# Four chained transformer layers on one core: another order and another way of loading in the two wide cross attentions

## The chip, the cores and the metric

The kernel runs on one core of one Trainium2 chip. The metric is the device time of one execution in microseconds (us), the median of several runs. A core has five engines that each work through their own list of instructions in order and wait for one another by semaphores: TensorE (PE; its weight loads are listed apart as PEld), VectorE (DVE), ScalarE (ACT), GpSimd (POOL) and SyncE (SP), which here only issues DMAs.

## The reference

Two sequences x of 1024 tokens by 256 features go through four layers; each layer has a self attention, a cross attention to 77 context tokens of 192 features, and an MLP. Layers 0 and 1 have 16 heads of 16 features ("narrow"), layers 2 and 3 have 16 heads of 64 ("wide"). In layer 2 a rope turns queries and keys. The part in which the change lies is the wide cross attention:

```python
def _attn(xq, ctx, wq, wkv, wo, bo):       # layer 2; layer 3 is the same without _rope
    q = _heads(xq @ wq)                    # 16 heads x 1024 x 64
    k, v = jnp.split(ctx @ wkv, 2, axis=-1)
    k = _heads(k); v = _heads(v)           # 16 heads x 77 x 64
    q = _rope(q, sq, cq)
    k = _rope(k, sk, ck)
    sim = jnp.einsum('bhnd,bhmd->bhnm', q, k) * DH ** (-0.5)
    a = jax.nn.softmax(sim, axis=-1)
    o = jnp.einsum('bhnm,bhmd->bhnd', a, v)
    return o.transpose(0, 2, 1, 3).reshape(xq.shape[0], xq.shape[1], MID) @ wo + bo
```

All is float32; products are made of split operands (a high and a low part, stacked along the contraction).

## The kernel before

The whole program is one launch. A planner, not the text of the program, sets the order. Every stage (one self attention, cross attention, key and value preparation "kv", or MLP of a layer) calls `plan.put(at, end, steps)`, where `at` is a time in the stage's own units; all steps of a stage are sorted by it, and then each engine's program is written by going through the one list and doing, for each step, what that engine has in it. So every engine works in the order of the list, and a step that waits holds up whatever stands behind it on that engine. Results of TensorE lie in PSUM banks, which are taken in turn from a small ring and given back by the engine that reads them.

**A unit of a wide cross attention.** `core64_steps` (its first loop) writes the steps of 32 units n. One unit is two heads times 512 queries:

- `cs` n, 0 and n, 1: scores of one head each, eight matmuls (L939, 128x256, the two heads of a pair). VectorE takes the maximum (L1716), ScalarE four exponentials of 128x77 with their sums (L1402).
- `cnorm` n: VectorE's reciprocal of the sums (L1725) and GpSimd's multiplication of all the unit's weights by it (L1939, 128x616).
- `cturn` n: TensorE transposes them (L1043, eight), ScalarE copies them out of PSUM (L1410, 77x1024).
- `cav` n: weights times values (L1055); `fin` n: ScalarE copies the output (L1391, 128x512).
- `proj` n: output projection (L1161, eight matmuls for a unit); VectorE adds it to x (L1769).

Before, their places relative to n are -1, -0.6, -0.3, 0.15, 0.65, 0.66 and 1.35.

**Queries.** Beside the units, `nat64` makes the queries of a group g of four heads, in two halves of 12 matmuls (L939, 128x512). There are eight groups; two of them are made ahead of the units, six among them, one for each four units (at 4g - 6.7 to 4g - 5.3). In layer 3 ScalarE copies such a block out of PSUM (L1335, high part) and VectorE forms its low part (L1631). In layer 2 it is turned by the rope first: ScalarE copies (L1347), VectorE multiplies by the cosine (L1644), GpSimd by the sine (L1926) and adds and subtracts the halves (L1932, L1933), ScalarE writes the high part (L1353) and VectorE the low one (L1651). `qstack` then moves the parts by DMAs of SyncE (L2102) into the stacks QS, of which there are three. `w_load` (L2002) brings a group's weights to a staging buffer and `w_split` (L1572, L1576 on VectorE) splits them.

**Keys and values.** The kv stage of layer 2 runs beside the MLP of layer 1, that of layer 3 beside the MLP of layer 2. It puts keys to DRAM as KXD (`kv_keep`, L2125, 616-byte rows) and values as VD (L2131). At the start of the cross attention `kv_stack` (L2136, L2143, L2147) loads from there the two key stacks KXA and KXB_, in which one key's parts are repeated on other partitions, and the values. In KXB_ a head uses half of the partitions and the other half has to be zero; VectorE clears it in `begin64` (L1595, L1596) after clearing parts of the query stacks (L1588, L1592) and the tail of the key tiles (L1594), and SyncE waits for that before L2143. TensorE waits for all key pieces (`kx_in`) before the first scores.

**Rope table.** `rope_load` (L2016) loads the table in layer 2 twice, once for the self attention and once for the cross attention into its own tile `S.CS`.

The lines that do the loading, before:

```python
for blk, s in enumerate((0, 1, 0, 1)):
    e.dma_start(f(S.KXA[32 * blk:32 * blk + 32, :, 0:NW]), KXD[s].rearrange("(h r) n -> r h n", r=32)
                ).then_inc(*kx_in.inc(S.i, 16))
w.wait_ge(zeroed, (S.i, "k"))
```

The norm of the following MLP (`norm_steps`, L1320, L1549, L960 and others) stands among the last units of each sequence.

## Time and profile before

| | |
|---|---|
| median of 3 runs | 4787.32 us (4774.97 to 4794.02) |
| profiled execution, its own time | 4777.17 us |
| its span in the profile | 4775.4 us |
| mean granted TensorE clock | 0.936 |
| busy: PE, DVE, ACT, POOL | 4153.2, 3084.2, 2077.1, 1344.1 us (87, 65, 43, 28%) |
| cross attention of layer 2 | about 2824 to 3207 us of the span |
| cross attention of layer 3 | about 4287 to 4620 us |

The profile is of one execution; times in it are microseconds from the span's start. In the rows below, a row of the timeline gives start, duration, engine, line, operation, what is written and read with its shape, how many instructions were put together (x8), and in brackets how long the engine was idle before and which instruction of which engine ended that. PEclk is the clock that TensorE was granted, as a share of the full 2.4 GHz; its lower level is 1.2 GHz. A wait is put down to the last releaser.

### The profile page before, as it was taken

What the parts mean: (1) busy time and instruction counts of PE and PEld (TensorE: products, weight loads), DVE (VectorE), ACT (ScalarE), POOL (GpSimd) and SP (SyncE); (2) the same over time, 40 slices, a digit from 0 to 9 for tenths busy, and PEclk for the clock granted to TensorE, in tenths of its full rate; (3) what the DMA queues carried; (4) which work ended last, traced back from release to release, by engine and by line L of the source; (5) the groups of instructions that cost most, each with busy time, mean ns of one, the idle gap of its engine ahead of it and who ended that gap; (6) DMA issues with size and microseconds to landing.
All of it is one profiled execution on the core that took longest, in us unless ns stands there. A gap on an engine that the chain in (4) does not pass through costs nothing. (4 is left out here: it accounts for less than half of the span.)

```text
span 4775.4 us, 56539 instructions
## 1 busy us (share of the span) xinstructions
PE 4153.2 (87%) x20828; PEld 2555.2 (54%) x20828; DVE 3084.2 (65%) x4628; ACT 2077.1 (43%) x3756; POOL 1344.1 (28%) x664
## 2 busy tenths in 40 slices
PE   6899989799998888888989877779799999987879
PEld 4343356634335665554555435658555555545668
DVE  4888856688885655666666754335577777773345
ACT  2555644255564433333333434544244344434541
POOL 1000001100001024555555543321243444441120
PEclk9999989899998989999999988889899999998989
DMA  4223231212323122221222224321322232226420
GB/s 120 31 52 47 42 56 34 49 28 48 45 42 61 33 60 66 56 58 40 62 62 58 59 67 92 86 64 32 81 70 67 59 69 62 57 42 135 91 60 18
DMA packets 155299, 282.01 MB, mean 59 GB/s; under 512 B 36186, under 2 KB 68244, under 8 KB 153872
## 3 DMA queue, kind: packets, MB, share of 16 engines
q1 hardware_dynamic: 155024, 278.40, 27.8%
q8 instruction: 166, 2.72, 0.2%
q14 instruction: 109, 0.89, 0.1%
HBM read 101.01 MB, written 25.23 MB: 26 GB/s over the span
## 5 line engine op out<-in xcount | busy, mean ns | idle before, releaser
L939 PE MATMUL PS<-t 128*128 128x512 f32 (+4 forms) x7896 | 2015.5, 387 | 232.0 <-ACT t L1381 99.3
L939 PEld LDWEIGHTS PS<-t 128*128 128x128 f32 (+2 forms) x7896 | 1264.1, 188 | 792.5 <-issue 256.2
L1381 ACT ACTIVATE t<-PS 128x512 f32<-128x512 f32 (+2 forms) x1600 | 1164.5, 750 | 1083.3 <-PE PS L939 1076.9
L1659 DVE TENSOR_REDUCE t<-PS 128x1 fp32r<-128x1024 f32 x512 | 621.8, 1220 | 304.1 <-PE PS L1011 298.1
L1119 PE MATMUL PS<-t 128*32 128x512 f32 (+2 forms) x4352 | 813.0, 613 | 0.2
L1663 DVE TENSOR_REDUCE t<-PS 128x1 f32<-128x512 f32 x1024 | 649.1, 682 | 76.1 <-PE PS L1015 74.7
L1952 POOL TENSOR_TENSOR t<-t 128x1024 f32<-128x1024 f32 x256 | 621.1, 2426 | 144.7 <-ACT t L1381 119.7
L1015 PE MATMUL PS<-t 96*128 96x512 bf16 x1024 | 375.0, 396 | 37.4 <-DMA t<-scr_n 13.5
L1011 PE MATMUL PS<-t 128*128 128x512 f32 x1024 | 339.4, 415 | 59.3 <-DMA t<-t 40.6
L1948 POOL TENSOR_TENSOR t<-t 128x1024 f32<-128x1024 f32 x64 | 155.5, 2430 | 743.4 <-PE PS L1129 462.7
L1890 POOL TENSOR_TENSOR t<-t 128x2048 f32<-128x2048 f32 x24 | 109.4, 4559 | 893.2 <-DMA t<-in_rows 560.4
L1119 PEld LDWEIGHTS PS<-t 128*32 128x32 f32 (+2 forms) x4352 | 171.2, 122 | 329.9 <-issue 325.6
L1161 PE MATMUL PS<-t 128*128 128x256 f32 x1024 | 282.4, 425 | 27.7 <-ACT t L1402 11.6
L1015 PEld LDWEIGHTS PS<-t 96*128 96x128 bf16 x1024 | 97.2, 97 | 374.7 <-DVE t L1663 155.9
L1769 DVE TENSOR_TENSOR t<-PS,t 128x1024 f32<-128x1024 f32 x128 | 156.4, 1222 | 211.1 <-PE PS L1161 211.1
L1011 PEld LDWEIGHTS PS<-t 128*128 128x128 f32 x1024 | 197.1, 197 | 125.4 <-DVE t L1659 31.7
L1161 PEld LDWEIGHTS PS<-t 128*128 128x128 f32 x1024 | 214.9, 216 | 70.2 <-issue 20.4
L1402 ACT ACTIVATE t<-PS,t 128x77 f32<-128x77 f32 x512 | 159.3, 324 | 182.2 <-DVE t L1716 182.2
L1748 DVE RECIPROCAL PS<-PS 128x256 f32<-128x256 f32 x128 | 224.7, 1755 | 12.5 <-PE PS L1129 12.5
L1249 PE MATMUL PS<-t 128*128 128x256 f32 x1536 | 217.1, 293 | 13.3 <-DVE t L1864 4.6
L1249 PEld LDWEIGHTS PS<-t 128*128 128x128 f32 x1536 | 205.9, 198 | 25.8 <-issue 10.1
L1939 POOL TENSOR_TENSOR t<-t 128x616 f32<-128x616 f32 x64 | 78.2, 1222 | 447.0 <-DVE t L1725 447.0
(135 smaller groups left out, 3982.0 us busy)
## 6 DMA issues: line engine op xcount, KB each, us to landing
t<-t SPq DMA_DIRECT2D x512, 128.0 KB, 3.6
t<-t SPq DMA_DIRECT2D x256, 256.0 KB, 3.9
t<-scr_n SPq DMA_DIRECT2D x288, 128.0 KB, 6.2
scr_n<-t SPq DMA_DIRECT2D x72, 256.0 KB, 2.2
t<-t SPq DMA_DIRECT2D x256, 64.0 KB, 2.0
t<-in_L_Wg SPq DMA_DIRECT2D x16, 768.0 KB, 4.6
t<-in_L_W SPq DMA_DIRECT2D x36, 256.0 KB, 3.2
t<-in_L_Wo SPq DMA_DIRECT2D x64, 128.0 KB, 2.6
```

The source lines that it names most:

```text
L939: ins = e.matmul(out, l, r, start=i == 0, stop=i == len(terms) - 1, tile_position=tp)
L1011: ins = e.matmul(o[:, 512 * h:512 * h + 512], u.smq[j][qt], u.smk[j][h], start=True, stop=True)
L1015: e.matmul(o, u.smq[j][qt], u.smk[j][half], start=True, stop=True).then_inc(*bank_full[k].inc(nth))
L1119: ins = e.matmul(banks[S.ot][wd * j:wd * j + wd, :], u.v[j][kt], P[0:S.pr, j, :], start=kt == 0, stop=kt == S.nkt - 1, tile_position=(0, w ...
L1161: ins = e.matmul(o[:, 256 * q:256 * q + 256], S.OR[n % 2][:, 128 * q:128 * q + 128], u.wo[:, :], start=True, stop=True)
L1249: ins = e.matmul(banks[4 + q][:, 0:D], l, r, start=m == 0 and t == 0, stop=m == 7 and t == 2)
L1381: e.activation(dst, src, ACT.Exp, scale=S.L.scale).then_inc(*expd.inc((S.i, i)))
L1402: ins = e.activation(S.PQ[n % 3][:, j, t, :], o[:, 256 * t + CT * b:256 * t + CT * b + CT], ACT.Exp, bias=S.NM[n % 3][:, at], accum_out=S. ...
L1659: e.tensor_reduce(S.MT[m % 2][:, qt, j:j + 1], o, AX.X, ALU.max, negate=True).then_inc(*bank_free[k].nth(nth))
L1663: e.tensor_reduce(S.NMX[:, 4 * j + qt, half:half + 1], o, AX.X, ALU.max).then_inc(*bank_free[k].nth(nth))
L1748: e.reciprocal(o[:, hs], o[:, hs]).then_inc(*recip_made.inc((S.i, n, h)))
L1952: e.tensor_tensor(S.AP_[:, :, :], S.AP_[:, :, :], P[1][:, :, :], ALU.add).then_inc(*pool_summed.inc((S.i, n, kt)))
```

## The change

Four things change.

1. The places of a unit's steps in both wide cross attentions become -1.25, -0.85, -0.45, 0, 0.5, 0.51 and 0.9.
2. In layer 2 the cross attention uses the rope table tile of the self attention, which is now laid out so that the tile survives; it is loaded once, and that load waits for the new signal `kx_stacked`. Tiles of the cross attentions move in SBUF for it.
3. The key stacks are put together in DRAM: a new step `kv_restack` at 14.2 of the kv stage copies KXD to KXAD and KXBD (eight DMAs from DRAM to DRAM, and in layer 2 two more that write zeros into KXBD from a small tile; layer 3 uses the same zeros). `begin64` no longer clears KXB_.
4. `kv_stack` is four steps, for heads 0 to 4, 5 to 8, 9 to 12 and 13 to 15, at -19.5, -8.9, 1 and 4. Each loads a slice of the two stacks from DRAM (all 128 partitions in one DMA); the first and the last also load the values of one sequence. `kx_in` is four signals and `vx_in` two, so that a unit waits for its own piece.

```diff
+    KXAD, KXBD = dram("scr_ka", (128, 16, 2 * CT)), dram("scr_kc", (128, 16, 2 * CT))
...
+            if L.rope:
+                C.CS, C.roped = first.CS, first.i
...
-            for at, step in ((-1, ("cs", S, u.n, 0)), (-0.6, ("cs", S, u.n, 1)), (-0.3, ("cnorm", S, u.n)),
-                             (0.15, ("cturn", S, u.n)), (0.65, ("cav", S, u.n)), (0.66, ("fin", S, u.n)),
-                             (1.35, ("proj", S, u.n, 0))):
+            for at, step in ((-1.25, ("cs", S, u.n, 0)), (-0.85, ("cs", S, u.n, 1)), (-0.45, ("cnorm", S, u.n)),
+                             (0, ("cturn", S, u.n)), (0.5, ("cav", S, u.n)), (0.51, ("fin", S, u.n)),
+                             (0.9, ("proj", S, u.n, 0))):
...
+        plan.put(14.2, 0, [("kv_restack", K)])
...
-                    if L.rope:
-                        plan.put(-19.8, 0, [("rope_load", S)])
-                    plan.put(-19.5, 0, [("kv_stack", S.kv)])
+                    for i, at in enumerate((-19.5, -8.9, 1, 4)):
+                        plan.put(at, 0, [("kv_stack", S.kv, i)])
...
-                kv_ready(w, S)
+                kv_ready(w, S, u.pi % 8 // 2)
...
-                w.wait_ge(vx_in, S.kv.i)
+                w.wait_ge(vx_in[u.part.b], S.kv.i)
...
                     for k in K.keys:
-                        e.memset(f(k[:, 16 * NW:16 * NW + 102]), 0.0)
-                    e.memset(f(K.KXB_[0:64, 1::2, :]), 0.0)
-                    e.memset(f(K.KXB_[64:128, 0::2, :]), 0.0).then_inc(*zeroed.inc((K.i, "k")))
+                        ins = e.memset(f(k[:, 16 * NW:16 * NW + 102]), 0.0)
+                    ins.then_inc(*zeroed.inc((K.i, "k")))
...
             elif what == "kv64_stats":
                 S, = a
+                e.memset(S.Z[:, :], 0.0).then_inc(*k_zero.inc(S.i))
...
             elif what == "rope_load":
                 S, = a
-                if not S.cross:
-                    K = kvs[S.L.i]
-                    w.wait_ge(kx_kept, K.i)
-                    for v in vx_kept:
-                        w.wait_ge(v, (K.i, 1))
+                K = kvs[S.L.i]
+                w.wait_ge(kx_stacked, K.i)
+                for v in vx_kept:
+                    w.wait_ge(v, (K.i, 1))
...
-            elif what == "kv_stack" and a[0].L.style == 64:
+            elif what == "kv_restack":
                 S, = a
+                if S.L.i == 2:
+                    w.wait_ge(k_zero, S.i)
+                    z = S.Z[:, :].rearrange("p (o n) -> p o n", o=1).broadcast_to([64, 8, 2 * CT])
+                    for odd in range(2):
+                        e.dma_start(KXBD[64 * odd:64 * odd + 64, 1 - odd::2, :], z).then_inc(*kx_stacked.inc(S.i, 16))
                 w.wait_ge(kx_kept, S.i)
                 for blk, s in enumerate((0, 1, 0, 1)):
-                    e.dma_start(f(S.KXA[32 * blk:32 * blk + 32, :, 0:NW]), KXD[s].rearrange("(h r) n -> r h n", r=32)
-                                ).then_inc(*kx_in.inc(S.i, 16))
-                w.wait_ge(zeroed, (S.i, "k"))
+                    e.dma_start(KXAD[32 * blk:32 * blk + 32, :, :], KXD[s].rearrange("(h r) n -> r h n", r=32)
+                                ).then_inc(*kx_stacked.inc(S.i, 16))
                 for blk, s in enumerate((2, 3)):
                     for odd in range(2):
                         src = KXD[s].rearrange("(h two r) n -> two r h n", two=2, r=32)[odd]
                         at = 32 * blk + 64 * odd
-                        e.dma_start(f(S.KXB_[at:at + 32, odd::2, :]), src).then_inc(*kx_in.inc(S.i, 16))
-                for i in range(2):
-                    w.wait_ge(vx_kept[i], (S.i, 1))
-                for b in range(NB):
-                    e.dma_start(S.VXS[b][:, :], VD[b]).then_inc(*vx_in.inc(S.i, 16))
+                        e.dma_start(KXBD[at:at + 32, odd::2, :], src).then_inc(*kx_stacked.inc(S.i, 16))
+            elif what == "kv_stack" and a[0].L.style == 64:
+                S, i = a
+                w.wait_ge(kx_stacked, S.i)
+                hs = slice((0, 5, 9, 13)[i], (5, 9, 13, 16)[i])
+                for K, D_ in ((S.KXA, KXAD), (S.KXB_, KXBD)):
+                    e.dma_start(f(K[:, hs, :]), D_[:, hs, :]).then_inc(*kx_in[i].inc(S.i, 16))
+                if i % 3 == 0:
+                    b = i // 3
+                    for j in range(2):
+                        w.wait_ge(vx_kept[j], (S.i, 1))
+                    e.dma_start(S.VXS[b][:, :], VD[b]).then_inc(*vx_in[b].inc(S.i, 16))
```

Lines after the change are 8 to 9 higher than before from L939 on (L1043 is L1052, L1161 is L1170, L1402 is L1411).

TensorE in layer 2, around the first query block of a group, from the transposes of one unit to those of the next. L1043 are the transposes, L939 with 128x256 scores, L939 with 128x512 the query block, L1055 the values, L1161 the projection. Before:

```order
L1043 MATMUL PS<-t 77x128 x8
L939 MATMUL PS<-t 128x512 x12
L1161 MATMUL PS<-t 128x256 x4
L939 MATMUL PS<-t 128x256 x8
L1055 MATMUL PS<-t 64x512 x2
L939 MATMUL PS<-t 128x256 x8
L939 MATMUL PS<-t 128x512 x12
L1043 MATMUL PS<-t 77x128 x8
```

After:

```order
L1052 MATMUL PS<-t 77x128 x8
L948 MATMUL PS<-t 128x256 x8
L948 MATMUL PS<-t 128x512 x12
L1064 MATMUL PS<-t 64x512 x2
L948 MATMUL PS<-t 128x256 x8
L1170 MATMUL PS<-t 128x256 x4
L1052 MATMUL PS<-t 77x128 x8
L948 MATMUL PS<-t 128x512 x12
```

The second scores now stand ahead of the first query block, the projection behind the next scores, and the second block behind the next transposes.

ScalarE in layer 2, at the two query blocks of the last group. L1347 is the copy of a query block, L1353 its high part after GpSimd's work, L1402 the exponentials of a head, L1410 the copy of the transposes, L1391 the copy of a unit's output. Before:

```order
L1410 ACTIVATE t<-PS 77x1024
L1347 ACTIVATE t<-PS 128x2x512
L1402 ACTIVATE t<-PS,t 128x77 x4
L1353 ACTIVATE t<-t 128x2x512
L1391 ACTIVATE t<-PS 128x512
L1402 ACTIVATE t<-PS,t 128x77 x4
L1347 ACTIVATE t<-PS 128x2x512
L1410 ACTIVATE t<-PS 77x1024
L1353 ACTIVATE t<-t 128x2x512
L1402 ACTIVATE t<-PS,t 128x77 x4
L1391 ACTIVATE t<-PS 128x512
```

After:

```order
L1419 ACTIVATE t<-PS 77x1024
L1411 ACTIVATE t<-PS,t 128x77 x4
L1356 ACTIVATE t<-PS 128x2x512
L1400 ACTIVATE t<-PS 128x512
L1362 ACTIVATE t<-t 128x2x512
L1411 ACTIVATE t<-PS,t 128x77 x4
L1419 ACTIVATE t<-PS 77x1024
L1356 ACTIVATE t<-PS 128x2x512
L1411 ACTIVATE t<-PS,t 128x77 x4
L1362 ACTIVATE t<-t 128x2x512
L1400 ACTIVATE t<-PS 128x512
```

The exponentials of the second head stand ahead of the first block's copy now, and the output copy of a unit stands behind the second block's high part.

SyncE at the start of layer 3's cross attention. scr_k, scr_ka and scr_kc are the keys in DRAM, scr_v the values, in_L_Wo the projection's weights, in_L_caWq those of the queries. Before:

```order
L2136 DMA t<-scr_k 32x16x154 x4
L2143 DMA t<-scr_k 32x8x154 x4
L2147 DMA t<-scr_v 77x1024 x2
L2063 DMA t<-in_L_Wo 128x256 x2
L2002 DMA t<-in_L_caWq 128x512
```

After:

```order
L2161 DMA t<-scr_ka 128x770
L2161 DMA t<-scr_kc 128x770
L2166 DMA t<-scr_v 77x1024
L2071 DMA t<-in_L_Wo 128x256 x2
L2011 DMA t<-in_L_caWq 128x512
```

Three DMAs take the place of ten ahead of the projection's weights; the rest is loaded later.

## Rows read from the trace of the kernel before

**Rows 1.** Windows, TensorE: stretch, PE busy (instructions), PEclk, DMA share, GB/s

```profile
2880.00:3200.00 320.00, 253.58 (x1273) 0.88 0.34 76
4330.00:4600.00 270.00, 227.47 (x1224) 0.92 0.41 89
```

**Rows 2.** Waits, TensorE in layer 2 (2800 to 3220): total, times, longest

```profile
PE PS L1043 <- POOL t L1939: 54.4, 23, 8.4
PE PS L1161 <- ACT t L1402: 11.6, 6, 1.9
```

**Rows 3.** Waits of TensorE in layer 3 (4240 to 4640)

```profile
PE PS L1043 <- POOL t L1939: 41.2, 24, 3.4
```

**Rows 4.** Timeline of TensorE, one unit of layer 3

```profile
4431.81 1.10 PE L1043 MATMUL PS<-t 128*77 128x128 f32 x8 [1.48 <-POOL t L1939]
4432.75 1.89 PE L1161 MATMUL PS<-t 128*128 128x256 f32 x8
4434.29 1.33 PE L939 MATMUL PS<-t 128*128 128x256 f32 x8
4435.55 1.08 PE L1055 MATMUL PS<-t 77*64 77x512 f32 x4
4436.56 1.24 PE L939 MATMUL PS<-t 128*128 128x256 f32 x8
4439.30 1.10 PE L1043 MATMUL PS<-t 128*77 128x128 f32 x8 [1.50 <-POOL t L1939]
```

**Rows 5.** Timeline of VectorE, ScalarE and GpSimd ahead of the transposes at 4431.81

```profile
4428.34 0.47 DVE L1716 TENSOR_REDUCE t<-PS 128x4 f32<-128x308 f32 x1
4428.84 0.33 ACT L1402 ACTIVATE t<-PS,t 128x77 f32<-128x77 f32 x1 [2.31 <-DVE t L1716]
...
4430.06 0.61 ACT L1391 ACTIVATE t<-PS 128x512 f32<-128x512 f32 x1
4430.26 0.20 DVE L1725 RECIPROCAL t<-t 128x8 f32<-128x8 f32 x1 [1.46 <-issue]
...
4430.54 1.21 POOL L1939 TENSOR_TENSOR t<-t 128x616 f32<-128x616 f32 x1 [6.70 <-DVE t L1725]
```

**Rows 6.** Timeline of ScalarE and GpSimd, first query block of a group in layer 2

```profile
3024.12 1.02 ACT L1347 ACTIVATE t<-PS 128x1024 f32<-128x1024 f32 x1 [1.81 <-PE PS L939]
...
3025.22 2.37 POOL L1926 TENSOR_TENSOR t<-t 128x1024 f32<-128x1024 f32 x1 [5.13 <-ACT t L1347]
...
3030.22 1.22 POOL L1939 TENSOR_TENSOR t<-t 128x616 f32<-128x616 f32 x1
```

**Rows 7.** Timeline of TensorE in the same group of layer 2, its waits

```profile
3034.52 3.27 PE L1161 MATMUL PS<-t 128*128 128x256 f32 x8 [1.93 <-ACT t L1402]
...
3044.33 1.14 PE L1043 MATMUL PS<-t 128*77 128x128 f32 x8 [3.07 <-POOL t L1939]
...
3053.50 1.10 PE L1043 MATMUL PS<-t 128*77 128x128 f32 x8 [1.53 <-POOL t L1939]
```

**Rows 8.** Timeline of SyncE and TensorE, start of layer 3's cross attention

```profile
4296.80 1.78 SPq L2143 DMA_DIRECT2D t<-scr_k  x4
...
4300.34 0.42 SPq L2002 DMA_DIRECT2D t<-in_L_caWq  x1
...
4309.26 10.30 PE L939 MATMUL PS<-t 128*128 128x512 f32 x40 [14.60 <-DVE t L1572]
```

**Rows 9.** Timeline of GpSimd and VectorE, start of layer 2's cross attention

```profile
2830.82 2.34 POOL L1926 TENSOR_TENSOR t<-t 128x1024 f32<-128x1024 f32 x1 [22.08 <-DMA t<-in_rope]
...
2833.49 1.23 DVE L1644 TENSOR_TENSOR t<-PS,t 128x1024 f32<-128x1024 f32 x1
```

**Rows 10.** Timeline of SyncE and VectorE beside the MLP of layer 1

```profile
1669.28 3.40 SPq L2125 DMA_DIRECT2D scr_k<-t  x4
...
1691.44 0.36 SPq L2016 DMA_DIRECT2D t<-in_rope  x1
...
1725.23 1.28 DVE L1644 TENSOR_TENSOR t<-PS,t 128x512 f32<-128x512 f32 x2
```

More of the change, by code:

```diff
@@ L261, in _build @@
     kx_kept = signal("kx_kept")
-    kx_in = signal("kx_in")
-    vx_in = signal("vx_in")
+    kx_stacked = signal("kx_stacked")
+    k_zero = signal("k_zero")
+    kx_in = [signal(f"kx_in{i}") for i in range(4)]
+    vx_in = [signal(f"vx_in{i}") for i in range(2)]
     vx_kept = [signal(f"vx_kept{i}") for i in range(2)]
@@ L344, in attention_tiles @@
                 S.P = [sbt(c, [128, S.nh, 512]) for _ in range(S.npb)]
+            if L.style == 64 and cross:
+                S.nnq, S.nqs, S.qw = 2, 3, N
+                S.NQ = [sbt(c, [128, 4, N], F32R) for _ in range(S.nnq)]
             S.OR = [sbt(c, [128, 512]) for _ in range(2)]
+            if L.rope and cross:
+                sbt(c, [128, 196])
+                sbt(c, [128, 2, N])
             S.R = [sbt(c, [128, 4, S.nh]) for _ in range(2)]
@@ L373, in attention_tiles @@
             if cross:
-                S.nnq, S.nqs, S.qw = 2, 3, N
-                S.NQ = [sbt(c, [128, 4, N], F32R) for _ in range(S.nnq)]
                 S.QS = [sbt(c, [128, 2, 2, S.qw], F32R) for _ in range(S.nqs)]
-                if L.rope:
-                    S.CS = sbt(c, [128, 2, N])
             elif not L.rope:
@@ L409, in kv_tiles @@
                 S.CS = sbt(c, [128, 2, 2 * CT])
+                S.Z = sbt(c, [64, 2 * CT])
                 S.T4 = [sbt(c, [128, 2 * CT]) for _ in range(4)]
@@ L467, in wide_layer @@
             attention_tiles(first, c)
+            first.roped = first.i
         with ExitStack() as c:
@@ L725, in _build @@
                     for at, step in ((7.9, "kv_load"), (9.1, "kv16"), (9.15, "kv_keep"), (9.9, "kv_stack")):
-                        plan.put(at, 0, [(step, K)])
+                        plan.put(at, 0, [(step, K) + ((0,) if step == "kv_stack" else ())])
                     if not L.i:
@@ L744, in _build @@
                 if S.cross:
-                    if L.rope:
-                        plan.put(-19.8, 0, [("rope_load", S)])
-                    plan.put(-19.5, 0, [("kv_stack", S.kv)])
+                    for i, at in enumerate((-19.5, -8.9, 1, 4)):
+                        plan.put(at, 0, [("kv_stack", S.kv, i)])
                 if S.cross:
@@ L919, in m_chunk, with kv_ready @@
         return stage, hi[:, at[0], at[1]], lo[:, at[0], at[1]], at
-    def kv_ready(w, S):
-        w.wait_ge(kx_in, S.kv.i)
+    def kv_ready(w, S, i):
+        w.wait_ge(kx_in[i], S.kv.i)
         w.wait_ge(zeroed, (S.kv.i, "k"))
@@ L1020, in tensor_program @@
                     w.wait_ge(s, key)
-                kv_ready(w, S)
+                kv_ready(w, S, 0)
                 o, k, nth = take(w, ring, ("max", S.i, m, j, q0))
@@ L1635, in vector_program @@
                 i = rope_order(S).index((S, g, qk, half))
-                w.wait_ge(rope_in, S.i)
+                w.wait_ge(rope_in, S.roped)
                 w.wait_ge(rope_copied, (S.i, i))
@@ L2166, in sync_program @@
             elif what == "kv_stack":
-                S, = a
+                S, _ = a
                 w.wait_ge(kx_kept, S.i)
```

5 lines of the change are left out of this document (2 added, 3 removed).

## The prediction

> **What bounds the kernel now.** I read the windows first: in the two wide cross attentions (layer 2, 2880 to 3200 us, and layer 3, 4330 to 4600) TensorE is busy 253.6 of 320 us and 227.5 of 270, at a mean granted clock of 0.88 and 0.92 [rows 1]. Then the waits: TensorE waits for GpSimd's L1939 before the transposes of L1043 for 54.4 us in layer 2 and 41.2 in layer 3, and in layer 2 for ScalarE's exponentials before the projection for 11.6 [rows 2, 3]. The timeline shows one unit n of layer 3: transposes of n, projection of n-1, second scores of n+1, values of n, first scores of n+2, then an idle 1.50 [rows 4]. The starts are 0.94, 1.54, 1.26, 1.01 and 1.24 apart, so a unit is 5.99 of work in a period of 7.49. The idle time is a latency: behind the second scores come max 0.5, four exponentials 1.4, reciprocal 0.3 and L1939 1.27, by the starts in [rows 5], against only values and first scores (2.25) on TensorE. So these stages are bound by TensorE plus this chain; the narrow layers, self attentions and MLPs aren't touched, except that a DRAM restack is put beside two MLPs.
>
> **The change, part by part.**
>
> *Longer lead.* In the new order the projection also lies between second scores and their transposes: values 1.01, first scores 1.24, projection 1.54 = 3.8 on TensorE against a chain of 3.3 to 3.5: the wait of a plain unit goes. What is late next: the projection of n needs L1391's copy of its output, which stands on ScalarE behind the exponentials of n+1. Max 0.5, exponentials 1.3, copy 0.6 [rows 5] end 2.4 after the second scores; TensorE gets there after 2.25. New wait 0.15 to 0.2 per plain unit.
>
> Layer 3: the units of a group (two blocks of 12 query matmuls each) need one more: VectorE does L1631 behind ScalarE's copy of the same 1024 elements (1.2 us like L1644 in rows 9, and 1.0 like L1347 in rows 6) before the max of the second scores, so exponentials end 3.9 after them and the copy 4.5 where TensorE is there after 2.25 plus the time before; followed, 1.25 per group. Six groups x 1.25 = 7.5, 24 plain units x 0.17 = 4; removed 41.2 [rows 3], but 3.4 of it belong to the start below, so the steady part is -37.8 + 11.5 = -26.3. For the layer norm that runs beside the last units I take -3.4, an estimate: its chain has less waiting between units to be spread over; bounds 0 and -7.
>
> Layer 2: here a query block is turned by GpSimd, and L1939 is queued behind it. The rows of before: copy 3024.12, GpSimd from 3025.22, three operations, L1939 at 3030.22 [rows 6], i.e. 5.0 us in which GpSimd gives nothing else. By the new order second scores (1.24) stand ahead of the first block, so from the transposes of unit 1 (t=0): scores end 2.2, block 5.05, copy 5.3 to 6.3, GpSimd 6.4 to 11.4, L1939, next transposes 12.7. TensorE has values, first scores and projection until 8.85, and waits 3.8, where before the second block covered it. Then the second block 13.8 to 16.7, GpSimd 17.95 to 22.95, L1353 to 24.0, L1391 to 24.6 behind it, projection at 24.65; TensorE has been through since 20.2: 4.45. Then 0.6 and three waits of 0.1 to 0.2. That makes 9.3 a group, for 1.93 + 3.07 + 1.53 + about as much again = 8.1 before [rows 7]. Six groups x 9.3 = 56, seven plain units x 0.2 and 2 for the norm (an estimate) = 3.4; removed 54.4 + 11.6, of which 8.4 at the start [rows 2]: -57.6 + 59.4 = +1.8. **The longer lead brings nothing in the groups of layer 2**: only its last seven units gain (about -10), and the groups give +7 back.
>
> *Clock.* After a wait the eight projection matmuls took 3.27 where a warm run shows 1.89 [rows 4, 7]: the array was at 1.2 instead of 2.4 GHz. A mean of 0.92 over 270 us is 43 us at the low level, of 0.88 over 320 is 77 [rows 1]; half of each is lost work at most, 21.6 and 38. Low bound of the give-back 0. In layer 3 the waits fall from 1.5 to 0.2 but three cold stretches (start, norm, ends) stay: I take -8. In layer 2 the long waits stay, two a group instead of two: -8 for the plain units and for what the 1.5 us waits did.
> The Trainium skill ("TensorE: Matmul & The Clock Gate", section "HAM oscillation — how this bites in real kernels") says that recurring idle gaps send the array back to half clock each time, and prices it at half the time spent there. Rows 4 and 7 agree that it follows idle time; by the rule layer 3, with its gaps gone, would get the whole 21.6, which is the first rival below.
>
> *Starts of the stages.* Layer 3: SP waits for VectorE's clearing of the key stack (L1595, L1596) and issues L2143 at 4296.80, the weights of the second group at 4300.34, and TensorE goes on at 4309.26 [rows 8]. Now nothing of the keys is cleared and only five DMAs stand ahead of the weights. Estimates from those rows: issued about 4289.5, landed about 4297.4, split by 4298.7, TensorE -10.5. The query stacks then come last: issued behind the weights one a 0.95, in place near 4308. And the third group's weights are issued only after 16 stack DMAs and the second key piece, at about 4313, where VectorE wants them; it stands until about 4320, which gives 3 to 4 back: -6.8 at the second transposes. Bounds 0 and -10.5.
> Layer 2: GpSimd waited for the rope table until 2830.82, VectorE came to L1644 at 2833.49 behind the clearing [rows 9]. Now the table is there and the two memsets of the key stack (2.7 us with their gaps, an estimate) are gone: -2.7 for the first block's chain and all behind it, -0.7 for the second unit. Bounds 0 and -4.
> The other key pieces are waited for at units 4, 8 and 12, 20 us and more after their issue: nothing.
>
> *Restack.* SP issues 10 DMAs more beside the MLP of layer 1 (two of zeros, eight of DRAM to DRAM) and 8 beside that of layer 2. Four of this kind took 3.40 of issue [rows 10], so 7 to 8.5, in a stretch where SP next has the last value store, the weights and the rope table. The table was issued at 1691.44, and VectorE first uses it at 1725.23 [rows 10]; even issued at 1700 it has 25 to land. No row shows a DRAM-to-DRAM copy; the nearest are the moves between DRAM and SBUF (scr_k, rows 8 and 10), whose issue alone is 0.45 to 0.85 each. I take 0; the upper bound is 5 in each of two places, the lower 0. VectorE's clearing of the zero tile is small and beside waits.
>
> **Sum.** Layer 3: -26.3 - 3.4 - 8 - 6.8 = -44.5. Layer 2: +1.8 - 8 - 3.4 = -9.6. Together -54. On the profiled run's own 4777.2 us that is 4723; the median of the runs is 10.1 above it, so I state **4733 us** (-1.1%).
>
> **Rivals.**
> A, *the clock comes back in full*. Place: both stages. For: in layer 3 a projection behind a wait of 1.5 us still took 1.89 [rows 4], the high level, so short waits alone do not lower it. Against: the long waits of layer 2 stay. Layer 3 21.6 instead of 8, layer 2 28 instead of 8: -88, 4699.
> B, *the chains of a group cost more than by hand*: in layer 2 both long waits are followed by low clock in the block and the projection (+2.5 x 6 = 15), in layer 3 the copy behind the block is late twice (+7.5) and the clock gives nothing (+8): -54 + 30.5 = -23, 4764. For it speaks that one more queued instruction on GpSimd or ScalarE moves every unit.
> C, *the change doesn't do what it says*: the wait moves whole from L1043 to L1161, since the projection follows a copy that is queued behind the same exponentials. For: L1161 already waits 1.93 in layer 2 [rows 7]. Against: 2.4 against 2.25 above. Starts alone: -10, 4777.
> D, *slower*: TensorE's clock falls in the denser stretches of both stages. Price: a share x more of 590 us at the low level costs 295 x; the gain of 54 is gone from x = 0.18, i.e. mean clocks of 0.79 and 0.83, and slower by over 0.5% from 0.26: +30, 4817. For: cold stretches follow whatever idle time is left. Against: busy stretches ran at the high level.
>
> **Chances.** Forecast 0.52 (alone 4708 to 4758), A 0.16, B 0.18, C 0.09, D 0.05. A measurement tells about 0.5%, 24 us, from no change. Faster by more: forecast, A and half of B, 0.77; within: the rest of B and C, 0.18; slower 0.05. The range that holds it 8 times in 10 reaches from A to B and half to C: 4690 to 4778.
>
> **What would show it.** Waits before the transposes gone in layer 3 (under 8 us from 41), new waits of the projection for ScalarE (10 to 12). In layer 2 some 20 to 25 before the transposes and 25 to 30 before the projection; the groups of four units still at 40 to 42 us, against 31 to 33 in layer 3. Granted clock over 0.94 in layer 3, and about 0.9 in layer 2. TensorE's second query block of layer 3 about 10 us earlier, the second transposes only 7. Rope multiply in layer 2's self attention at its old place. If layer 2's groups come out at 36, my queue of GpSimd and ScalarE was wrong; if layer 3's stay at 34, the longer lead was.

## The result and the profile after

The changed kernel takes 4760.85 us (median of 10 runs, 4752.16 to 4768.35) against 4783.66 before (10 runs): a ratio of 0.9948 with a 95% interval of 0.9937 to 0.9959. So it is faster by 0.5%, 23 us, where 54 had been forecast; the stated range, 4690 to 4778, holds it.

The two profiled executions differ by less, 4768.35 against 4777.17, and a comparison of them alone would mislead. What can be compared is the length of each stage. A stage is measured between two of VectorE's additions of a projection to x (L1769, after L1777): the self attention from its first to its 31st, a cross attention from the last one (the 32nd) of the self attention ahead of it to its own last one. The windows of the kernel before, with columns as in [rows 1], are for the self attention of layer 2, the cross attention of layer 2 and that of layer 3:

```profile
1876.06:2807.64 931.58, 826.41 (x3464) 0.96 0.26 56
2822.27:3205.94 383.67, 281.29 (x1376) 0.84 0.39 87
4285.59:4619.16 333.57, 265.95 (x1376) 0.88 0.45 96
```

The same three of the kernel after:

```profile
1883.62:2823.17 939.55, 831.80 (x3464) 0.95 0.26 55
2837.61:3223.31 385.70, 280.27 (x1376) 0.84 0.38 85
4307.11:4611.42 304.31, 264.43 (x1376) 0.92 0.49 108
```

Layer 3's cross attention is 29.3 shorter, layer 2's 2.0 longer, and the self attention of layer 2, in which no instruction of the units is changed, 8.0 longer. The first of these rows also starts 7.6 later. TensorE's busy time in layer 3 fell only by 1.5 although the mean granted clock rose from 0.88 to 0.92. By these means, an estimate, TensorE was granted the low level for some 80 us before and 49 after, so nearly all of the low clock that went had lain in idle time.

TensorE's waits in layer 3's cross attention after (4290 to 4630), which answer to [rows 3]:

```profile
PE PS L1170 <- ACT t L1400: 17.7, 17, 2.6
PE PS L969 <- DVE t L1558: 7.8, 3, 3.9
...
PE PS L948 <- DVE t L1581: 3.5, 1, 3.5
PE PS L1052 <- POOL t L1948: 3.4, 2, 3.2
...
PE PS L1064 <- ACT t L1419: 2.6, 10, 1.1
```

and in layer 2's (2820 to 3240), which answer to [rows 2]:

```profile
PE PS L1170 <- ACT t L1400: 33.5, 15, 4.7
PE PS L1052 <- POOL t L1948: 29.9, 7, 8.4
```

In layer 3 the 41.2 before the transposes are 3.4, and a new wait of 17.7 stands before the projection, for the copy of the unit's output. In layer 2 the sum of the two waits is 63.4 where it was 66.0. There is a third one there, once, which the kernel before does not have:

```profile
2940.18 3.35 PE L1170 MATMUL PS<-t 128*128 128x256 f32 x8 [3.77 <-DMA t<-in_L_Wo]
```

The projection's weights for this unit are issued behind the fourth piece of the key stacks and the second sequence's values, and the new places want them earlier. The wait is 2.1 to 3.8 in the four profiles that have the new loading, the new places and the blocks at their old place; in three more with the blocks moved a wait of 3.1 to 3.8 stands at this place, for which the profile names no releaser. The profiles with only one of the two have none. This timeline of TensorE shows one group of layer 2 (to be read beside [rows 7]):

```profile
3053.07 1.99 PE L1052 MATMUL PS<-t 128*77 128x128 f32 x8 [3.56 <-POOL t L1948]
3054.71 5.97 PE L948 MATMUL PS<-t 128*128 128x512 f32 x20
...
3067.48 3.78 PE L1170 MATMUL PS<-t 128*128 128x256 f32 x8 [4.64 <-ACT t L1400]
```

GpSimd and ScalarE in the same group: 

```profile
3050.57 1.26 POOL L1942 TENSOR_TENSOR t<-t 128x512 f32<-128x512 f32 x1
3051.79 1.22 POOL L1948 TENSOR_TENSOR t<-t 128x616 f32<-128x616 f32 x1
...
3065.89 1.06 ACT L1362 ACTIVATE t<-t 128x1024 fp32r<-128x1024 f32 x1 [2.09 <-POOL t L1942]
3066.85 0.58 ACT L1400 ACTIVATE t<-PS 128x512 f32<-128x512 f32 x1
```

Both waits of a group are there as forecast (3.8 and 4.45 expected, 3.56 and 4.64 seen), each directly behind GpSimd's turning of a block. But 20 matmuls behind the first wait take 5.97, where they take 3.95 at the high clock, and the projection behind the second 3.78, where a warm one takes 1.89: both ran at the low clock, in whole or in part. The last groups are 41.8 and 43.9 long, from one such wait to the next; before they were 40.9.

And this is the start of layer 2's self attention after, where the prediction put the restack at nothing: SyncE, then VectorE and TensorE.

```profile
1678.46 6.75 SPq L2139 DMA_DIRECT2D scr_v<-t  x2
1685.25 1.29 SPq L2146 DMA_DIRECT2D scr_kc<-t  x2
1686.59 4.46 SPq L2149 DMA_DIRECT2D scr_ka<-scr_k  x4
1691.10 4.82 SPq L2155 DMA_DIRECT2D scr_kc<-scr_k  x4
1695.96 1.88 SPq L2139 DMA_DIRECT2D scr_v<-t  x1
1697.95 0.52 SPq L2011 DMA_DIRECT2D t<-in_L_Wg  x1
```

```profile
1708.66 0.96 DVE L1581 CAST t<-t 128x1536 fp32r<-128x1536 f32 x1 [5.23 <-DMA t<-in_L_Wg]
```

```profile
1714.03 1.12 PE L969 MATMUL PS<-t 128*128 128x128 f32 x4 [8.39 <-DVE t L1558]
1714.79 2.91 PE L1258 MATMUL PS<-t 128*128 128x256 f32 x12
```

The ten DMAs of the restack stand between the third and the fourth value store (10.6 us of issue), so the self attention's first weights are issued at 1697.95; before, at 1689.54. VectorE stands 5.2 us for them, with the norm's L1558 queued behind, and TensorE 8.39 for that norm, where it waited 3.40 before.

The 8.4 us of later issue are not what VectorE waits for. These are the issues of the weights by size and time from issue to landing, before and after:

```profile
t<-in_L_Wg SPq DMA_DIRECT2D x1, 768.0 KB, 5.4
```

```profile
t<-in_L_Wg SPq DMA_DIRECT2D x1, 768.0 KB, 10.7
```

VectorE was ready for them at 1703.4. Issued at 1697.95 and landing in 5.4 as before, they would have been there at 1703.4. They landed in 10.7, behind the data of the eight copies that stood ahead of them (308 KB each in four, 154 in the others). So nearly the whole wait of 5.2 is the time that the copies themselves took.

### The profile page after: what moved, and what is told of

Its sections match the earlier page's. It is cut to its first block and busy times, and to the rows that moved or that the text cites. A ratio compares the mean times of both kernels' runs of the same rounds, so it can differ in the third digit from the quotient of the medians.

```text
span 4766.6 us, 56541 instructions
## 1 busy us (share of the span) xinstructions
PE 4157.7 (87%) x20828; PEld 2548.7 (53%) x20828; DVE 3079.0 (65%) x4625; ACT 2080.2 (44%) x3756; POOL 1344.8 (28%) x664
## 5 line engine op out<-in xcount | busy, mean ns | idle before, releaser
L1170 PE MATMUL PS<-t 128*128 128x256 f32 x1024 | 284.3, 427 | 69.7 <-ACT t L1400 51.1
L1170 PEld LDWEIGHTS PS<-t 128*128 128x128 f32 x1024 | 211.5, 213 | 119.5 <-ACT t L1400 63.8
L1777 DVE TENSOR_TENSOR t<-PS,t 128x1024 f32<-128x1024 f32 x128 | 156.6, 1223 | 169.8 <-PE PS L1170 169.6
L1411 ACT ACTIVATE t<-PS,t 128x77 f32<-128x77 f32 x512 | 159.3, 324 | 105.9 <-DVE t L1724 105.8
L1873 DVE TENSOR_TENSOR t<-t 128x512 fp32r<-128x512 f32 x128 | 112.8, 882 | 128.2 <-ACT t L1493 127.0
```

The lines of the kernel that those rows point to most:

```text
L1170: ins = e.matmul(o[:, 256 * q:256 * q + 256], S.OR[n % 2][:, 128 * q:128 * q + 128], u.wo[:, :], start=True, stop=True)
L1411: ins = e.activation(S.PQ[n % 3][:, j, t, :], o[:, 256 * t + CT * b:256 * t + CT * b + CT], ACT.Exp, bias=S.NM[n % 3][:, at], accum_out=S. ...
```

## Experiments

The theory after the first comparison, T: layer 3's new places are worth less than forecast because of the wait for L1400; layer 2's cost a little, because of the order on GpSimd; the restack costs about 7 through the queue of SyncE (whose issue, and not the landing, this theory had in mind); and the rest of the difference between the two profiles is chance. The rivals are in the expectations.

### The places alone

```diff
 (the kernel before)
-            for at, step in ((-1, ("cs", S, u.n, 0)), (-0.6, ("cs", S, u.n, 1)), (-0.3, ("cnorm", S, u.n)),
-                             (0.15, ("cturn", S, u.n)), (0.65, ("cav", S, u.n)), (0.66, ("fin", S, u.n)),
-                             (1.35, ("proj", S, u.n, 0))):
+            for at, step in ((-1.25, ("cs", S, u.n, 0)), (-0.85, ("cs", S, u.n, 1)), (-0.45, ("cnorm", S, u.n)),
+                             (0, ("cturn", S, u.n)), (0.5, ("cav", S, u.n)), (0.51, ("fin", S, u.n)),
+                             (0.9, ("proj", S, u.n, 0))):
```

> The kernel before with the seven new places of a unit's steps and nothing else of the change. Theory T (from the two traces): the places are worth about -23 us in layer 3's cross attention and cost about 4 in layer 2's, and layer 2's self attention starts where it did, so 4762 to 4768 on a median of 4784 for before. Rival R (the places are worth my forecast, and the loading eats half of it): about 4740. In the trace under T: groups of four units of layer 2 at 42 to 44 us with a wait of 3.6 before the transposes and 4.6 before the projection; the first use of the rope table in layer 2's self attention at its old 1725.

Measured: 4763.18 against 4782.40, ratio 0.9955 (0.9938 to 0.9971), as T said; R's 4740 did not come. Its windows of the two cross attentions:

```profile
2822.23:3208.95 386.72, 282.42 (x1376) 0.83 0.39 86
4288.47:4596.66 308.19, 256.92 (x1376) 0.92 0.49 104
```

The places are worth -25.4 in layer 3 and +3.0 in layer 2. The undisturbed groups of layer 2 are 41.8 to 43.9. TensorE's busy time in layer 3 is 256.9, 9.0 under that of before and 7.5 under that of the changed kernel: with the places alone the clock does give something back there.

### The loading alone

The changed kernel with that edit undone.

```diff
 (the kernel after)
-            for at, step in ((-1.25, ("cs", S, u.n, 0)), (-0.85, ("cs", S, u.n, 1)), (-0.45, ("cnorm", S, u.n)),
+            for at, step in ((-1, ("cs", S, u.n, 0)), (-0.6, ("cs", S, u.n, 1)), (-0.3, ("cnorm", S, u.n)),
...
```

> The changed kernel with the old seven places: only the restack in DRAM, the loads in pieces and the rope table that stays. Theory T: +7.5 at the start of layer 2's self attention, because its first weights are issued 8 us later behind the restack's DMAs, -2.7 at the start of layer 2's cross attention and -7 to -11 at that of layer 3: together -2 to -6, within 0.2% of before. Rival R, the extra DMAs also slow the self attention of layer 2 all along (its end was 16 us late in the trace of the changed kernel, not 7.5): slower than before by 5 to 10 us. In the trace: VectorE's wait for the weights of about 5 us near 1703 to 1709, and the self attention of layer 2 as long as before from its first unit on (T), or 8 to 9 us longer (R).

Measured: 4787.82 against 4782.40, ratio 1.0008 (0.9995 to 1.0021): no difference that these runs tell. Windows:

```profile
1873.29:2806.62 933.33, 827.53 (x3464) 0.96 0.26 56
2821.08:3203.32 382.24, 278.54 (x1376) 0.85 0.39 86
4283.10:4613.74 330.64, 271.06 (x1376) 0.88 0.46 99
```

The loading shortens the cross attentions by 1.4 and 2.9. VectorE waits 4.3 for the first weights of layer 2's self attention, and the addition of that stage's first projection comes 179.8 behind the norm's reciprocal, where it was 173.1 before: 6.7 lost. The sum is +2.4, within the interval. T's 7 to 11 in layer 3 did not come: the first addition of a unit's projection is 5.8 earlier in the stage, but TensorE is busy for 271.1 instead of 266.0, and 2.9 are left. The self attention itself is 933.3 long, so R, a lasting slowdown, is out.

### The restack behind the weights

```diff
-        plan.put(14.2, 0, [("kv_restack", K)])
+        plan.put(17.2, 0, [("kv_restack", K)])
```

> The changed kernel with the restack's DMAs placed behind the last value store and the first weights of the next self attention (place 17.2 instead of 14.2 of the key and value stage). Theory T: VectorE's wait for these weights goes and with it 7 to 7.5 us: 4753 against 4761 for the changed kernel, ratio to before 0.9935. The rope table is then issued about 1708 to 1712 and VectorE wants it at 1725, so nothing new is late. Rival R1: the copies from DRAM to DRAM take bandwidth, not a place in the queue, and the weights land late all the same, no gain. Rival R2: the rope table becomes late, and gives 2 to 5 back.

Measured: 4756.55 against 4782.40, ratio 0.9942 (0.9925 to 0.9960); 4.3 under the changed kernel, which the intervals (they overlap) do not tell from it. The trace does. SyncE, the landing of the weights, VectorE and TensorE:

```profile
1687.69 0.36 SPq L2011 DMA_DIRECT2D t<-in_L_Wg  x1
...
1689.42 6.63 SPq L2149 DMA_DIRECT2D scr_ka<-scr_k  x4
...
1709.39 0.37 SPq L2024 DMA_DIRECT2D t<-in_rope  x1
```

```profile
t<-in_L_Wg SPq DMA_DIRECT2D x1, 768.0 KB, 6.3
```

```profile
1701.20 0.91 DVE L1581 CAST t<-t 128x1536 fp32r<-128x1536 f32 x1
```

```profile
1706.90 1.11 PE L969 MATMUL PS<-t 128*128 128x128 f32 x4 [3.42 <-DVE t L1558]
1707.66 2.91 PE L1258 MATMUL PS<-t 128*128 128x256 f32 x12
```

VectorE's wait is gone and TensorE's is 3.42 as before. The weights land in 6.3 with the copies right behind them, in 10.7 to 11.9 with the copies ahead (six profiles), and in 5.4 to 5.5 without copies (three). So R1, that they land late wherever they stand, is out: copies behind them cost about 1 us and copies ahead 5 to 6.5. But what the place ahead costs is the copies' own transfer and not their issue: in the six profiles, with a landing of 5.4 no wait would have been left. The first projection comes 177.3 behind the reciprocal, against 180.4. The rest of the way to 173.1 goes with the low clock behind the same wait (12 matmuls in 2.91 instead of 1.68), which the second profile of the kernel before has as well (177.6, below). The rope table, issued at 1709.39, holds nothing up (R2 out).

### The new places in layer 3 only

```diff
+            places = ((-1, -0.6, -0.3, 0.15, 0.65, 0.66, 1.35), (-1.25, -0.85, -0.45, 0, 0.5, 0.51, 0.9))[S.L.i == 3]
+            for at, step in zip(places, (("cs", S, u.n, 0), ("cs", S, u.n, 1), ("cnorm", S, u.n), ("cturn", S, u.n),
+                                         ("cav", S, u.n), ("fin", S, u.n), ("proj", S, u.n, 0))):
```

> The changed kernel with the new places in layer 3's cross attention and the old ones in layer 2's. Theory T: the new places lose about 4 in layer 2, so this is 3 to 5 us faster than the changed kernel, about 4757. Rival R (a plain unit of layer 2 does gain, and the low clock in the blocks of the trace is chance): 5 to 10 slower than the changed kernel. In the trace under T: the groups of layer 2 at 40.9 us again, those of layer 3 at 31.7 to 33.5.

Measured: 4755.03 against 4782.40, ratio 0.9937 (0.9921 to 0.9954). Layer 2's cross attention is 384.0, between the 385.7 of the changed kernel and the 382.6 of its second profile, its last groups 40.9 again, layer 3's 304.0. So the new places are worth nothing in layer 2, or cost up to 4; the difference of 6 in the medians is at the edge of what this tells.

### Layer 2's query blocks out of GpSimd's way

```diff
-                        plan.put(o + 2.3, o + 3.7, nat64_steps(S, g, 0))
+                        steps = nat64_steps(S, g, 0)
+                        places = (1.56, 2.25, 2.56, 2.58, 3.25, 3.56) if L.rope else (1.56, 2.56)
+                        if not (L.rope):
+                            places = [2.3 + 1.4 * i / len(steps) for i in range(len(steps))]
+                        for at, step in zip(places, steps):
+                            plan.put(o + at, 0, [step])
```

> The changed kernel with the six query blocks of layer 2's cross attention moved so that GpSimd's turning of a block stands behind the multiplication of the unit it used to hold up: first block at o+1.56, its additions at 2.25, its low part at 2.56, second block one unit later (2.58, 3.25, 3.56); before 2.3 to 3.7. The same work, one unit earlier. Theory T: the groups of layer 2 are long (42 to 47 us) only because of the order on GpSimd and ScalarE: the waits of 3.6 and 4.6 a group fall under 1 each, the blocks and projections behind them run at the high clock, a group is 31 to 34, and the kernel 55 to 75 us faster than the changed one: 4686 to 4706. Rival R1 (the turning itself, 5 us of GpSimd and 2.1 of ScalarE a block, is too much for the time between two units wherever it stands, since the PSUM buffers and the one buffer of the turned block hold TensorE): groups of 38 to 41, 4731 to 4745. Rival R2 (the stacks' DMAs or the weights of the next group come late as the blocks come early): waits of TensorE or VectorE for a DMA, gain under 20.

Measured: 4713.70 against 4785.13, ratio 0.9838 (0.9819 to 0.9858), 47 under the changed kernel. The window of layer 2's cross attention, and TensorE in one group of it:

```profile
2840.64:3175.03 334.39, 261.44 (x1376) 0.90 0.44 98
```

```profile
3026.15 1.89 PE L1175 MATMUL PS<-t 128*128 128x256 f32 x8
...
3031.73 3.98 PE L953 MATMUL PS<-t 128*128 128x512 f32 x20
3035.54 1.89 PE L1175 MATMUL PS<-t 128*128 128x256 f32 x8
```

No wait before the transposes is left but the first (8.4), the 20 matmuls with a block take 3.98 instead of 5.97, and a group is 32.8 instead of 41.8 to 44. R1, that the turning is too much work wherever it stands, is out: GpSimd does exactly the same work. So is R2, a gain under 20; of it a wait of 3.1 is left before one projection, whose releaser the profile does not name. A group with the norm of the next part in it is longer than 32.8. The gain of 51 in the stage, and of 47 in the kernel, is under T's 55 to 75, as 16.9 of waits before the projection are left, the longest 4.6.

### The same in layer 3

```diff
+                        if not (not L.rope):
```

The same edit with this condition, i.e. for layer 3 alone.

> The changed kernel with the query blocks of layer 3's cross attention at o+1.56 and o+2.56 instead of 2.3 and 3.0, i.e. behind the copy of a unit's output on ScalarE and between values and next first scores on TensorE. Theory T: the wait of 1.5 a group for the output's copy, which stood behind VectorE's low part, the max and the exponentials, goes, and with it the low clock of the projection behind it (3.6 instead of 1.99): 1.5 to 3 a group in six groups, 9 to 15 us faster than the changed kernel: 4746 to 4752. Rival R: the copy is late anyway, as ScalarE now does the block's copy ahead of the exponentials of the next unit: 0 to 3 us.

Measured: 4747.54 against 4785.13, ratio 0.9917 (0.9900 to 0.9934), 13 under the changed kernel. The wait for the output's copy and the window:

```profile
PE PS L1175 <- ACT t L1405: 5.6, 11, 1.2
```

```profile
4304.23:4599.51 295.28, 257.13 (x1376) 0.94 0.51 111
```

The wait fell from 17.7 to 5.6 and the stage from 304.3 to 295.3, busy time from 264.4 to 257.1: here too the clock gives something, with the waits of 1.5 gone. These waits have two prices in the changed kernel, as its projections in layer 3 show:

```profile
4396.94 3.68 PE L1170 MATMUL PS<-t 128*128 128x256 f32 x8 [1.49 <-ACT t L1400]
...
4443.88 1.99 PE L1170 MATMUL PS<-t 128*128 128x256 f32 x8 [1.48 <-ACT t L1400]
```

Equal waits of 1.49 and 1.48 are followed by 3.68 at the low clock once and by 1.99 at the high one the other time; groups of 33.5 and of 31.8 us are the two cases, and the profile does not show what decides between them.

### All three

```diff
-        plan.put(14.2, 0, [("kv_restack", K)])
+        plan.put(17.2, 0, [("kv_restack", K)])
...
-                        plan.put(o + 2.3, o + 3.7, nat64_steps(S, g, 0))
+                        places = (1.56, 2.25, 2.56, 2.58, 3.25, 3.56) if L.rope else (1.56, 2.56)
+                        for at, step in zip(places, nat64_steps(S, g, 0)):
+                            plan.put(o + at, 0, [step])
```

> Both moves of the blocks and the restack behind the first weights of the next self attention. If the three causes are separate the gains add up: T 4676 to 4700 from 55 to 75 in layer 2, 9 to 15 in layer 3 and 4 at the start of layer 2's self attention. Rival: 10 us or more of them are lost where one stage's end meets the next stage's start, or to a lower clock in denser stretches (mean clock under 0.9 there).

Measured: 4697.57 against 4785.13, ratio 0.9813 (0.9793 to 0.9834), a version that beats both kernels. 63 under the changed kernel, where the three alone gave 47, 13 and 4. Stage windows:

```profile
2829.93:3169.94 340.01, 265.90 (x1376) 0.89 0.44 96
...
4247.68:4543.49 295.81, 257.71 (x1376) 0.94 0.51 111
```

Layer 2's is 5.6 longer than with its blocks moved alone (groups of 34.1 instead of 32.8), and the clock explains it: behind the same wait of 1.2 once a group, the projection takes 3.48 to 3.64 here in four of five groups and 1.99 there. The range of T held; that the gains add up is shown only to within that.

### The output's copy by VectorE

```diff
 (on top of all three; TensorE's waits for the copy read o_outv in these stages)
+            elif what == "fin" and a[0].cross and a[0].L.style == 64:
+                ...
+                e.tensor_copy(S.OR[n % 2][:, :], banks[n % 2]).then_inc(*o_outv.inc((S.i, n)))
```

> The kernel of e7 with the copy of a unit's output in the two wide cross attentions done by VectorE, which has nothing queued between the second head's maximum and the next one's, instead of by ScalarE, where it stands behind four exponentials. Theory T: what is left of the projection's waits for this copy (16.1 us in layer 2 and about 6 in layer 3) is the queue on ScalarE: the waits fall under 3 in each stage, 12 to 20 us faster than e7: 4678 to 4686. Rival R: the reciprocal or the maximum behind the copy on VectorE moves the wait back to the transposes, no gain or a loss of 5.

Measured: 4694.38 against 4784.03, ratio 0.9805 (0.9784 to 0.9827); its interval covers the ratio of the three edits alone. The expected 12 to 20 did not come, nor a loss. In layer 2 (2780 to 3200) and layer 3 (4200 to 4560) TensorE's waits are

```profile
PE PS L952 <- ACT t L1415: 17.8, 18, 1.6
```

```profile
PE PS L952 <- ACT t L1415: 10.5, 15, 1.2
```

where they were 6.5 and 7.6 with the copy on ScalarE. The projection no longer waits for the copy, but now the next scores wait for the PSUM buffer that ScalarE's exponentials give back. In layer 2 all of the gain is lost (342.2 against 340.0), in layer 3 4.1 of it stays (291.7 against 295.8). Neither T nor R as I had put it: the wait moved on to the scores, not back to the transposes.

### Old places in layer 2, blocks moved

```diff
+            places = ((-1, -0.6, -0.3, 0.15, 0.65, 0.66, 1.35), (-1.25, -0.85, -0.45, 0, 0.5, 0.51, 0.9))[S.L.i == 3]
...
-                        places = (1.56, 2.25, 2.56, 2.58, 3.25, 3.56) if L.rope else (1.56, 2.56)
+                        places = (1.72, 2.45, 2.71, 2.73, 3.45, 3.71) if L.rope else (1.56, 2.56)
```

> The kernel of e7 with the old places of a unit's steps in layer 2's cross attention, the query blocks still behind the multiplication of a unit (first block at o+1.72, the rest in step). Theory T: once the blocks are out of GpSimd's way the longer lead is worth what it is in layer 3, the wait of 1.5 a unit: with the old places the groups of layer 2 are 36 to 38 instead of 33, the kernel 20 to 30 us slower than e7: 4718 to 4728. Rival R: the gain came from the blocks alone and the lead is worth nothing in layer 2: within 5 us of e7.

Measured: 4705.79 against 4784.03, ratio 0.9848 (0.9820 to 0.9875): 8 slower than all three, where T said 20 to 30; the intervals overlap. Layer 2's cross attention is 348.7 against 340.0, and 334.4 with its blocks alone moved. In it

```profile
PE PS L1055 <- POOL t L1951: 40.0, 20, 8.4
```

is back, but the groups are only 33.9 to 35.3. Against 384 before, the blocks' place alone brings 35 in layer 2 and the longer lead 9 to 14 more; without the blocks' move the lead had brought nothing. So T's size was wrong. R, that the lead is worth nothing once the blocks are moved, is contradicted by the length of the stage, one profile here against two, and not by the medians.

### Second profiles of both kernels

> The kernel before, unchanged, for a second profile. Layer 2's self attention took 931.6 us from its first to its 31st projection in one profile and 939.6 after the change, with the same instructions. Theory T (chance of the clock): it varies by 10 us or more among profiles of one kernel, and its length goes with the granted clock of the stage. Rival R: it is 930 to 934 in every profile of this kernel, and longer only with the new loading. The cross attentions 382 to 386 in layer 2 and 332 to 336 in layer 3 by both.

> The changed kernel, unchanged, for a second profile. T: VectorE's wait for the first weights of layer 2's self attention of 5 us again, the first projection of that stage 6 to 8 late against the stage's norm, but the stage from there 928 to 945 long as chance has it; cross attentions 384 to 388 and 302 to 306. R: the stage is 939 or more again.

Measured: 4800.06 and 4747.48 in these executions. The self attention of layer 2 in the second profile of the kernel before, then in the second of the kernel after:

```profile
1882.26:2826.33 944.07, 838.02 (x3464) 0.94 0.26 55
```

```profile
1879.56:2810.80 931.24, 825.41 (x3464) 0.96 0.26 56
```

944.1 and 931.2, where the first profiles had 931.6 and 939.6: the stage varies by 13 with the granted clock, in both kernels, so T holds and the 8.0 of the first comparison are chance. The rest varies less. VectorE's wait for the weights is 4.9 again, and the first projection 179.9 behind the norm (179.8 to 180.4 in the six profiles with the restack at 14.2; 173.1, 173.2 and 177.6 in the three with the old loading; 172.7 to 177.3 in the four with the restack behind the weights). The cross attentions are 382.6 and 304.1 after, 384.2 and 336.8 before.

## Why the prediction came out too large

By stages, with the mean of both profiles: layer 3's cross attention 335.2 to 304.2, -31.0 (forecast -44.5); layer 2's 383.9 to 384.1, +0.2 (forecast -9.6); start of layer 2's self attention +7, or +5 against the mean of the three old ones (forecast 0). That is -24 to -26, and the medians say -23. A stage is TensorE's busy time and its idle time, and both can be set against the terms of the sum. Three steps failed:

1. **The clock, 12.** "I take -8" in each stage. Busy time fell by 2.4 in layer 3 (266.7 to 264.3) and 1.7 in layer 2 (281.6 to 279.9). The bound took half of all time at the low clock as lost work, but most of that time was idle time, in which a low clock costs nothing. In layer 2 the long waits made blocks cold that had been warm (12 matmuls took 3.00 there before). In layer 3 the 8 was right for the places by themselves, which freed 9.0 (one profile); the new loading took it back: up to the units' first query block TensorE is busy for 38.9 in the changed kernel and for 35.2 with the places alone, and for 3.8 more in the rest of the stage. Nothing in the sum had the earlier start of the stage cost clock.
2. **New waits, 8 in layer 3 and 3.5 in layer 2.** In layer 3 the removed waits were as forecast, 41.2 - 3.4 = 37.8. Instead of the 11.5 put in against them, the projection's wait grew by 16.9 (17.7 from 0.8), 2.6 came before the values for ScalarE's copy of the transposes and 1.3 before scores for the exponentials, neither of which was in the sum: 20.8. Behind a block the projection waited 1.5, in a plain unit up to 0.5 and once at the start 2.6, where 1.25 and 0.15 to 0.2 had been taken. The norm's waits fell by 1.2 instead of 3.4. Together that is 11.5; idle time at the start of the stage fell by 4 more than the 6.8 put in, which leaves 8 (idle 68.5 to 39.9). In layer 2 idle time rose by 1.9 where it should have fallen by 1.6: the two waits worked out came out close, and 2.4 and 1.3 of the same small waits came on top, and 2.1 to 3.8 for the projection's weights. These weights stand behind the key pieces in the queue, of which the prediction says "nothing", having followed the pieces to their consumer and not what stands behind them.
3. **The restack, 5 to 7.** "I take 0", with a bound of 5. The rope table's slack was worked out, and it was enough; the first weights in the same queue were named and not followed, and of the copies only the issue was priced. The weights were issued 8.4 later, which their slack would just have covered, and took 10.7 instead of 5.4 to land behind the copies, which it did not. The later restack shows it. In the second place, ahead of layer 3's self attention, VectorE waits 1.1 to 3.6 for the same reason, and the first projection comes 158.4 to 159.3 behind the norm in five profiles and 162.0 in one, against 158.3: about 1.

These make 29 to 31 of the 31 missing, so that little is left for chance; what the stages vary is as large as the last of them.

**What held.** Start of layer 3: the second group's weights were issued and split where forecast, TensorE's wait for them fell from 14.6 to 3.5 (11.1 for 10.5), and VectorE stood 5.9 for the third group's weights, as forecast. The loss set against it came too: measured against the run with the places alone, the second transposes are 8.0 earlier in the stage and the units' first query block 6.8, where 6.8 had been put in. Of these 6.8 only 3.9 are left at the end of the stage, because of item 1. Start of layer 2: -2.8 to L1652, the stage as a whole 1.4 by the run with the loading alone. Layer 2's groups: waits of 3.56 and 4.64 for 3.8 and 4.45, and the place of the fault named, GpSimd's queue. Of the signs that were to show the forecast, the waits before the transposes came, the groups nearly (41.8 to 43.9 for 40 to 42, 31.8 to 33.5 for 31 to 33), the projection's wait in layer 3 (17.7 for 10 to 12) and the granted clock (0.92 for over 0.94 in layer 3, 0.84 for about 0.9 in layer 2) did not.

Rivals A, C and D did not occur. B's mechanism came true in part: the low clock behind both waits of a group in layer 2, the clock giving next to nothing in layer 3 and the copy late there. That the result, 4761, lies at B's 4764 is luck for the rest, since B put 15 on layer 2's groups, of which the stage shows 10 in all, and had no restack in it.

Behind the waits of 3.6 and 4.6 in layer 2 TensorE was at the low clock; behind six waits of 1.5 in layer 3 it was there three times and three times not. The Trainium skill ("TensorE: Matmul & The Clock Gate", section "HAM oscillation — how this bites in real kernels") says that recurring idle gaps send the array back to half clock. The traces agree for the long gaps, and for the short ones only in part.

## What to carry to other kernels

A longer lead on one engine moves the wait to whatever stands next in another engine's queue: write down, for each consumer, what its producer has queued ahead of it, and move the large rare work (here the turning of a query block) behind the small urgent one. That move of twelve blocks a layer was worth 47 us in layer 2 and 13 in layer 3 (where it put them behind the copy of a unit's output), the lead itself 25 in layer 3 and in layer 2 nothing until the blocks had moved. When transfers are added to the list that one engine issues, follow every transfer behind them to its consumer, not only the one that is touched, and give it the time that the added data take to move besides the time of their issue: here the second was the one that hurt. And price a low clock on busy time, not on elapsed time.

## What the runs showed of the hardware

- Copies from DRAM to DRAM, of which the trace of before had none: the eight of them took 9.3 us of SyncE to issue (4.46 and 4.82), and 11.9 in the later place. The rope table, whose load waits for them and for the values, followed 11.3 after the last of them was issued (1695.92 to 1707.21), 8.0 in the later place (1701.38 to 1709.39).
- A load of 768 KB issued by SyncE landed in 5.4 to 5.5 us without these copies (three profiles), in 6.3 to 6.6 with them right behind it (four) and in 10.7 to 11.9 with them ahead of it (six). What stands ahead counts, what stands behind hardly does.
- After the same wait of 3.40 us TensorE ran on at the high clock in one execution of the kernel before and at the low one in another (12 matmuls 1.68 or 2.91). That stage's first projection came 4.4 us later against its norm in the second execution, of which 2.6 were lost in the first three rows behind the wait.
- After a wait of 1.2 us, once a group, the projection took 1.99 in one kernel's profile and 3.48 to 3.64 in another's with the same order of work in that stage, which made the stage 5.6 us longer.
- Layer 2's self attention, the same instructions in all thirteen profiles, was 928.6 to 948.0 us long; the longest had the lowest mean clock (0.94). So a single pair of profiles can't be compared at their ends. Lengths of the other stages repeat better: the cross attentions of one kernel agreed within 3.2 us between its two profiles.
